# An expert stage in tiles of 256 tokens instead of 128, with quarters of its two products in turn on TensorE

## What is computed

```python
probs = softmax(h_flat @ router_w)
gates, idx = top_k(probs, 2)
hid  = relu(einsum('nd,edf->nef', h_flat, exp_w1) + exp_b1)   # d = 256, f = 1024
eout = einsum('nef,efd->ned', hid, exp_w2) + exp_b2
y    = einsum('ned,ne->nd', eout, combine)                    # two experts for each token
```

## Time and profile before

| | us |
|---|---|
| runs: median (lowest to highest of 3) | 1499.03 (1496.92 to 1502.69) |
| the profiled execution | 1499.17 |
| its span on the core | 1497.0 |
| routing stage, to the first matmul of line 489 | 0 to 172.1 |
| expert stage, to the last matmul of line 507 | 172.1 to 689.0 (516.9 long) |
| busy: PE, DVE, ACT, POOL | 1295.6, 1138.4, 963.0, 738.3 |

### The profile page before, as it was taken

The page is one execution under the profiler, slowest core; times in us unless marked ns, Lnnn a source line. Parts: engine busy times, 40 slices in busy tenths (PEclk is TensorE's granted clock), DMA queues, the critical chain, the costliest instruction groups (busy, mean ns, idle before and its releaser), DMA issues. The chain is left out here.

```text
span 1497.0 us, 36973 instructions
## 1 busy us (share of the span) xinstructions
PE 1295.6 (87%) x9225; PEld 1126.6 (75%) x9225; DVE 1138.4 (76%) x3159; ACT 963.0 (64%) x2326; POOL 738.3 (49%) x645
## 2 busy tenths in 40 slices
PE   2666499999999999994579999999999999999996
PEld 2555388888888888883468878888788877788875
DVE  3888799999999999995657666676666775666652
ACT  2222388888888888881166666666666666676671
POOL 1677488888888888884212323223232332322211
PEclk9999999999999999996799999999999999999997
DMA  3676333333433434344666665566655566555520
GB/s 115 210 239 221 125 133 127 126 126 126 134 127 125 128 124 135 127 127 141 202 222 191 215 190 184 168 189 211 196 182 172 185 210 204 175 184 167 184 78 14
DMA packets 197678, 241.07 MB, mean 161 GB/s; under 512 B 20720, under 2 KB 176560, under 8 KB 197616
## 3 DMA queue, kind: packets, MB, share of 16 engines
q1 hardware_dynamic: 184816, 202.70, 42.9%
q10 hardware_dynamic: 6624, 20.84, 4.3%
q0 software_dynamic: 6176, 16.79, 3.2%
HBM read 196.36 MB, written 39.71 MB: 158 GB/s over the span
## 5 line engine op out<-in xcount | busy, mean ns | idle before, releaser
L351 POOL TENSOR_TENSOR w_lo<-w,w_hi 128x512 fp32r<-128x512 f32 x284 | 422.7, 1518 | 100.2 <-ACT w_hi L412 100.2
L1176 ACT ACTIVATE bias<-bias,neg_max 128x256 f32<-128x256 f32 x512 | 255.3, 501 | 200.8 <-DVE neg_max L1488 200.3
L714 DVE TENSOR_TENSOR w_lo<-w,w_hi 128x512 fp32r<-128x512 f32 x284 | 302.0, 1102 | 1.0 <-ACT w_hi L406 1.0
L412 ACT ACTIVATE w_hi<-w 128x512 fp32r x284 | 179.2, 632 | 54.0 <-PE ps_y L507 35.8
L1488 DVE CUSTOM_DVE_ANT_0 bias<-ps_s,bias 128x256 f32<-128x256 f32 x512 | 194.2, 416 | 20.2 <-PE ps_s L1264 13.1
L406 ACT ACTIVATE w_hi<-w 128x512 fp32r x284 | 173.3, 632 | 21.7 <-DVE tile_tab L683 11.0
L1128 POOL TENSOR_TENSOR act_lo<-up_f,act_hi 128x512 fp32r<-128x512 f32 x64 | 82.5, 1289 | 209.3 <-ACT act_hi L1220 209.3
L507 PE MATMUL ps_y<-w_hi,hidT_hi 128*128 128x256 f32 x568 | 168.8, 297 | 14.8 <-DVE hidT_lo L700 14.2
L1262 PE MATMUL ps_s<-mask_f,minus_ident 128*128 128x256 f32 x512 | 155.4, 325 | 28.4 <-DVE neg_max L1488 15.9
L1276 PE MATMUL ps_p<-const,bias 128*128 128x128 f32 x1024 | 157.5, 277 | 13.7 <-ACT bias L1176 13.6
L507 PE MATMUL ps_y<-w_hi,hidT_lo 128*128 128x256 f32 x568 | 161.7, 285 | 0.0
(11 more groups left out here) (266 smaller groups left out, 3330.3 us busy)
## 6 DMA issues: line engine op xcount, KB each, us to landing
bias<-bias_dram SPq DMA_DIRECT2D x128, 512.0 KB, 3.8
b_row<-b_dram SPq DMA_DIRECT2D x71, 512.0 KB, 3.6
w<-w_dram ACTq DMA_DIRECT2D x32, 512.0 KB, 4.7
xin<-dispatch SPq DMA_DIRECT2D x71, 128.0 KB, 2.2
b_row<-b_dram SPq DMA_DIRECT2D x71, 128.0 KB, 3.1
expert_out<-xin SPq DMA_DIRECT2D x71, 128.0 KB, 1.7
q_stack<-q_hi_rows SPq DMA_DIRECT2D x64, 128.0 KB, 2.9
k_stack<-k_hi_rows SPq DMA_DIRECT2D x64, 128.0 KB, 2.9
```

Of the source, the lines that this page charges most:

```text
L351: pool.tensor_tensor(w2_part["lo"][:, k, :], w2_piece(e, k), w2_part["hi"][:, k, :].bitcast(F32), ALU.subtract).then_inc(sem("w2_split"), 1)
L412: act.activation(w2_part["hi"][:, k, :], w2_piece(e, k), ACT.Copy).then_inc(sem("w2_upper"), 1)
L714: dve.tensor_tensor(w1_part["lo"][:, k, :], w1_piece(e, k), w1_part["hi"][:, k, :].bitcast(F32), ALU.subtract).then_inc(sem("w1_split"), 1)
L1176: act.activation(head_rows(h, j), head_rows(h, j), ACT.Exp, scale=-1.0, bias=neg_max[par][:, h, j:j + 1], accum_out=total[par][:, h, j:j + ...
```

## The change

A tile has TOK = 256 rows, and `TILES` becomes (8192 - 256) // 256 + 8 = 31 + 8 = 39. The expert stage is written anew around that:

- **First product.** The weights are now stationary and the 256 tokens move, so the hidden values come out transposed, 128 hidden features on the partitions: 8 outputs `f` of 128x256, two in each of four PSUM banks `ps_h`. `turn_hidden` is gone. Bias and relu are one ACT instruction for each f (128x256), with the bias as a column (`b1` lies in SBUF once for all experts).
- **Hidden halves.** ACT writes float32 to SBUF; DVE rounds a pair of f (128x512) to the hi half and makes the lo half of the even pairs, GpSimd makes the lo half of the odd pairs.
- **Order.** Both products are cut in four quarters `k` of 12 matmuls of 256 columns. TensorE runs up(t, 0), down(t-1, 0), up(t, 1), turn_in(t+1), down(t-1, 1), up(t, 2), down(t-1, 2), up(t, 3), down(t-1, 3). There is still one buffer for each weight piece, one `htokT` (now twice as wide) and one set of hidden halves.
- **Before the stage.** 8 blocks of 256 instead of 128 zero rows pad the regions of `dispatch`; small weights of the routing stage lie in the last expert's place in `w1` until ACT loads it, and ACT waits once for them; the tables of tiles are made in `columns` and are 39 entries long.

```diff
+TOK = 256
-TILES = (K * B * T - P) // P + E
+TILES = (K * B * T - TOK) // TOK + E
...
+        def lower_hidden(t, g):
+            wait_alone(pool, sem("hid_rounded"), 2 * t + g // 2 + 1)
+            lower_pair(pool, t, g).then_inc(sem("hidT_odd"), 1)
...
+                lower_hidden(t, 1)
+                lower_w2(t, e, 0)
+                lower_w2(t, e, 1)
+                lower_hidden(t, 3)
+                lower_w2(t, e, 2)
+                lower_w2(t, e, 3)
...
             act.wait_ge(sem("tile_turned"), t + 1)
-            wait_free(act, sem("w1_used"), PARTS * t)
-            act.activation(htokT["hi"][:], ps_t[:, 0:C * P].rearrange("p (c m) -> p c m", c=C), ACT.Copy).then_inc(sem("htokT_upper"), 1)
+            wait_free(act, sem("up_done"), F * t)
+            act.activation(htokT["hi"][:], ps_t[:, :].rearrange("p (c m) -> p c m", c=C), ACT.Copy).then_inc(sem("htokT_upper"), 1)
+
+        def relu(t, e, f):
+            if f % 2 == 0:
+                g = f // 2
+                wait_alone(act, sem("up_done"), F * t + f + 2)
+                wait_free(act, sem("hidT_odd" if g % 2 else "hidT_even"), 2 * t + g // 2, alone=True)
+            act.activation(hid[:, f % HID_SLOTS, :], ps_h[f // 2][:, (f % 2) * TOK:(f % 2 + 1) * TOK], ACT.Relu,
+                           bias=b1[:, bass.ds(e, 1), f:f + 1].rearrange("p e f -> p (e f)")).then_inc(sem("hid_ready"), 1)
+
+        def upper_w1(t, e, k):
+            wait_free(act, sem("up_done"), F * (t - 1) + 4 * (k // C + 1), alone=True)
...
+        def upper_w2(t, e, k):
+            wait_free(act, sem("w2_used"), PARTS * (t - 1) + k + 1, alone=True)
...
+            for k in range(PARTS):
+                if a_tile(t):
+                    relu(t, e, 2 * k)
+                    relu(t, e, 2 * k + 1)
+                    upper_w2(t, e, k)
+                if a_tile(t + 1):
+                    if k == 1:
+                        upper_w1(t + 1, ahead, 0)
+                        upper_w1(t + 1, ahead, 1)
+                    if k == 3:
+                        take_in(t + 1)
+                        upper_w1(t + 1, ahead, 2)
+                        upper_w1(t + 1, ahead, 3)
...
+        def up(t, k):
+            if k == 0:
+                pe.wait_ge(sem("htokT_split"), t + 1)
+            if k % 2 == 0:
+                pe.wait_ge(sem("w1_split"), PARTS * t + k + C)
+            wait_free(pe, sem("hid_ready"), F * (t - 1) + 2 * k + 2)
...
+        def down(t, k):
+            if k == 0:
+                wait_free(pe, sem("y_ready"), t)
+            pe.wait_ge(sem("w2_split"), PARTS * t + k + 1)
+            pe.wait_ge(sem("hidT_odd" if k % 2 else "hidT_even"), 2 * t + k // 2 + 1)
...
+        def split_hidden(t, g):
+            dve.wait_ge(sem("hid_ready"), F * t + 2 * (g + 1))
+            wait_free(dve, sem("w2_used"), PARTS * (t - 1) + g + 1)
...
+            rounded = dve.tensor_copy(hidT["hi"][:, rows, :], hid[:, slots, :])
...
+            for k in range(PARTS):
+                if a_tile(t):
+                    split_hidden(t, k)
+                if a_tile(t + 1) and k == 1:
+                    lower_w1(t + 1, e, 0)
+                    lower_w1(t + 1, e, 1)
             if a_tile(t + 1):
                 lower_tokens(t + 1)
+            if a_tile(t - 1):
+                take_out(tile.ahead(-1))
+            if a_tile(t + 1):
                 lower_w1(t + 1, e, 2)
                 lower_w1(t + 1, e, 3)
```

More of the change, by code:

```diff
@@ L285, in body @@
                 load(tile.ahead(2))
-                load_b1(tile.ahead(2))
             if a_tile(tile.t - 1):
-                store(tile.t - 1)
+                store(tile.ahead(-1))
             if a_tile(tile.t + 1):
@@ L292, in _ @@
         load(Tile(0, 0))
-        load_b1(Tile(0, 0))
         tile_loop(sp, body)
-        sp.wait_ge(sem("y_sent"), 16 * TILES)
+        for par in range(2):
+            sp.wait_ge(sem(f"y_sent{par}"), 16 * ((TILES + 1 - par) // 2))
     @block.gpsimd
@@ L477, in turn_in @@
             for c in range(C):
-                last = pe.transpose(ps_t[:, c * P:(c + 1) * P], htok[tile.par][:, c * P:(c + 1) * P], ident)
+                for j in range(J):
+                    last = pe.transpose(ps_t[:, c * TOK + j * P:c * TOK + (j + 1) * P], htok[tile.par][:, j, c * P:(c + 1) * P], ident)
             last.then_inc(sem("tile_turned"), 1)
[L481 to L491, removed]
@@ new lines, in down @@
+        def down(t, k):
[3 more added lines that the diff above has]
+            pe.wait_ge(sem("hidT_odd" if k % 2 else "hidT_even"), 2 * t + k // 2 + 1)
+            for f in (2 * k, 2 * k + 1):
+                for j in range(J):
+                    for n, (a, b) in enumerate(PASSES):
+                        last = pe.matmul(ps_y[j][:, 0:D], hidT[a][:, f, j * P:(j + 1) * P],
+                                         w2_part[b][:, k, (f % 2) * D:(f % 2 + 1) * D],
@@ L508, in down @@
                                          start=(f == 0 and n == 0), stop=(f == F - 1 and n == 2))
-                last.then_inc(sem("w2_used"), 1)
+            last.then_inc(sem("w2_used"), 1)
         def body(tile):
             t = tile.t
-            if a_tile(t - 1):
-                turn_hidden(t - 1)
-            if a_tile(t):
-                up(t)
-            if a_tile(t + 1):
-                turn_in(tile.ahead(1))
-            if a_tile(t - 1):
-                down(t - 1)
+            for k in range(PARTS):
+                if a_tile(t):
+                    up(t, k)
+                if a_tile(t + 1) and k == 1:
+                    turn_in(tile.ahead(1))
+                if a_tile(t - 1):
+                    down(t - 1, k)
@@ L725, in take_out @@
             dve.wait_ge(sem(f"b2_in{tile.par}"), 16 * (tile.before + 1))
-            wait_free(dve, sem("y_sent"), 16 * t)
-            dve.tensor_tensor(y, ps_y[:, 0:D], b2[tile.par][:], ALU.add).then_inc(sem("y_ready"), 1)
+            wait_free(dve, sem(f"y_sent{tile.par}"), 16 * tile.before)
+            for j in range(J):
+                last = dve.tensor_tensor(y[tile.par][:, j, :], ps_y[j][:, 0:D], b2[tile.par][:], ALU.add)
+            last.then_inc(sem("y_ready"), 1)
         def body(tile):
```

182 lines of the change are left out of this document (84 added, 98 removed).

## The result

| | before | after |
|---|---|---|
| runs: median (lowest to highest of 4) | 1497.97 (1496.63 to 1502.69) | 1576.93 (1575.15 to 1577.77) |
| span of the profiled execution | 1497.0 | 1576.0 |
| start of the expert stage | 172.1 | 175.2 |
| its length | 516.9 | 590.6 |
| from its end to the end of the span | 808.0 | 810.2 |

The changed kernel takes 1.052 times as long (95% interval 1.0493 to 1.0546): 79 us more. Of these 3.1 lie before the expert stage, 73.7 in it and 2.2 behind it.

A forecast was written before the change was run, and what follows sets the result against it. VectorE and TensorE were both full; afterwards TensorE's 11.95 us plus a 2.40 us hand-over pause set a 14.35 us beat. With the ends this gave 1546.7 us, plus 20 for clock falls: 1567 us, range 1538 to 1594.

The forecast's parts named there:

- The pause: Between tiles in the expert stage: TensorE waits for the new tokens behind ScalarE's fourth second-weights piece, 2.40 us per tile.
- The beat: Time per 256-row tile in the expert stage: 11.95 us of TensorE work plus 2.40 us of pause, 14.35 us.
- The clock: TensorE's clock in the expert stage: one tile in three falls, 13 falls of 1.5 us, 20 us more; chance 0.50.
- The sum: Expert stage 561.2 us from first tile, 37 beats, last tile and cold start; whole kernel 1546.7 us at full clock.
- cold start: Start of the expert stage: TensorE begins at half clock, as before, 1.7 us.
- wait of about 1: Last tile: a wait of about 1 us beside its own second product of 5.7 us, within the 18.5 us forecast.
- The rounding copy: VectorE's copy of 128x512, four per tile: taken as 0.6 us each, bounded by 0.34 and 1.37, 2.4 us together.
- unless the pause is gone: Rival that VectorE sets the beat: even at 13 us it lies under 14.35, so it moves nothing while the pause stands.
- Tokens in time: Rival at the tile border: ScalarE passes line 429 early, tokens are ready, kernel faster or equal; chance 0.05.
- Clock unaffected: Rival in the expert stage: the pause leaves TensorE's clock alone, 1547 us; chance 0.32.
- Every tile falls: Rival in the expert stage: TensorE's clock falls in all 39 tiles, 58 us, 1605 us; chance 0.08 (every tile or nearly).
- Without the pause at all: Case of the tokens-in-time rival: no pause between tiles, beat 11.95 us, time 1458 us.

## Why the prediction was right, point by point

1567 was forecast, 1538 to 1594 as the range, slower by a chance of 0.94; 1577 came.

- **The pause.** The links forecast from the start of the last matmul of line 535 to the first of line 522 add up to 2.41 us; measured 2.53, of which 2.25 idle ("about 2.3"). By links: 0.47 for the notice as forecast, the piece with its step 0.53 (0.63 forecast), the hi half 0.62 with its way to VectorE (0.58), the lo half 0.69 (0.68), and 0.22 to TensorE where 0.05 was taken; the piece came 0.10 shorter and the last link 0.17 longer, so that the errors partly cancel. The order as its cause is shown by two runs: moving ScalarE's copy alone brings 30 us, and the same order in the old tiles costs 170.
- **The beat.** Forecast 14.35 at full clock, measured 14.43: the 0.1 by which the chain is longer. TensorE's work of 11.95 us is confirmed by the kernels without the pause, whose beats are 12.0 to 12.2.
- **The clock.** Forecast 13 falls of 1.5 us, measured 15 beats that are 1.53 longer, one of them by the long fall of the first tile, and a short fall more in the last tile. The filled pause shows it apart: 19 us. How many would fall was a guess between none and all; that it came near is luck. The prediction also took from the Trainium skill (TensorE: Matmul & The Clock Gate, section on HAM oscillation) that every step pays; here 15 of 37 pauses did. The kernel in that section waits for 3 to 5 us at each step, longer than the 2.25 us here, so its rule did not promise a fall for a pause of this length.
- **The sum.** The profiled spans differ by 79.0 us, where the forecast had 67.8. Of the 11 missing, the 37 beats are 6: 556.8 for 531 + 20, half from the longer chain and half from two more falls. The ends were priced too low by the other half. The first tile took 13.3 from one lo half of tokens to the next, where 10 and 1.7 for the cold start were taken (1.6 short; the relu, priced at 0.367 by a copy of that shape, took 0.471 on the mean, at most 0.8 us for eight). The last took 20.4 from its first matmul at 745.4, where 18.5 was (1.9 short): it holds the sixteenth fall, not counted, and 1.25 us of waiting at 759.85 for the results of the tile before, the "wait of about 1". The stage began 3.1 later instead of 2.2, and what follows it took 2.2 more instead of 1. Two small sums of the text do not close: 11.5 + 5.7 + 1 is 18.2 and not 18.5, and 11 us below 1547 is 1536 and not 1538. Neither decides anything.
- **VectorE.** The rounding copy was guessed at 0.6 and the mean is 0.695, a mixture of 0.42 and 1.51. The lo halves of the first weights took 1.52 on the mean instead of 1.11, since more of their time lay beside GpSimd; those of the hidden pairs, taken as "of the same kind", 0.69. The prices made no difference here, as the text said: "unless the pause is gone". In the repaired kernels it became the next bound.
- **The rivals.** Tokens in time: excluded by 80.6 us of waiting. Clock unaffected: excluded by 15 falls. Every tile falls: excluded by the 22 pauses that no fall followed. Without the pause at all the text gave 1458; with two buffers 1482 came, because the bound passed to VectorE beside GpSimd, and with GpSimd's work cut 1467.

## What to carry to other kernels

When an operand of the next step is made by an in-order engine, look at what stands ahead of it there: one piece that waits for the end of the present step turns a covered hand-over into a serial chain, here of 2.25 us in each tile. Mend it on every engine of the chain at once (ScalarE alone brought 30 us, with VectorE 53, with a second buffer 95), and expect the next bound behind it. If a pause of TensorE can't be removed, filling it with matmuls whose result nobody reads may pay, here 19 us.

## What the runs showed of the hardware that was not expected

- VectorE's copy of 128x512 from SBUF to SBUF takes 0.42 us alone and up to 1.51 beside a GpSimd tensor_tensor, 3.6 times as long. It ends 0.28 us after GpSimd's instruction whatever its own start, so it is held and not slowed. The lo half of 128x512 out of PSUM took 0.68 to 0.69 beside GpSimd or alone.
- Between stretches of some 12 us of unbroken work, a pause of 2.0 to 2.3 us was followed by a fall of TensorE's clock in 15 of 37 cases, one of 1.6 to 1.85 us in 5 of 37, one of 1.2 to 1.5 us in none of 37. Sixteen transposes of a constant in the pause, which left 0.5 us of it idle, prevented all 15, so that work for nothing made the kernel 19 us faster.
- With two more copies for each tile in ScalarE's body, unrolled by four, packets appear on the instruction queue at each turn of the loop (43 instead of 6), and the turn takes 1.3 to 2.2 us beyond the usual beat. Unrolled by two, both are gone. That these packets are code loaded again is the theory that forecast this; whose code they carry the profile does not say.
